# Expert loop of a fused layer: gate transposes ahead of the second-layer pass, and differences that read the largest values in place

## The reference, cut to what matters

```python
z = jnp.einsum('nd,sdr->nsr', xf, P)
scores = jnp.einsum('nsr,smr->nsm', z, C)
topv, topi = jax.lax.top_k(scores, K)
w = jax.nn.softmax(topv, axis=-1)
h = jax.nn.gelu(jnp.einsum('nsr,nskrh->nskh', z, W1g) + b1g)
yl = jnp.einsum('nskh,nskhr->nskr', h, W2g) + b2g
comb = jnp.einsum('nskr,nsk->nsr', yl, w)
out = jax.nn.gelu(comb @ G1 + g1b) @ G2 + g2b
```

## Time and profile before

| what | value |
|---|---|
| three runs | 931.4, 931.75, 930.24 us |
| median | 931.4 us |
| profiled execution: its own time / span in the profile | 930.38 / 928.5 us |
| PE busy | 882.7 us (95%) |
| DVE busy | 676.9 us (73%) |
| ACT busy | 568.1 us (61%) |
| POOL busy | 474.8 us (51%) |
| mean granted TensorE clock | 0.985 |

### The profile page before, as it was taken

How to read it: one execution, slowest core, us unless ns; L and a number is a source line. 1 busy time by engine, 2 the same in 40 slices (tenths; PEclk the granted TensorE clock), 3 DMA queues, 4 the chain that set the end, 5 groups by cost and what they waited for, 6 DMA issues and landing times.

```text
span 928.5 us, 16150 instructions
## 1 busy us (share of the span) xinstructions
PE 882.7 (95%) x5422; PEld 396.3 (43%) x5422; DVE 676.9 (73%) x1681; ACT 568.1 (61%) x844; POOL 474.8 (51%) x445
## 2 busy tenths in 40 slices
PE   8899999999999989899999999999999999899997
PEld 3477777777677756222222222322232222222222
DVE  6566655665576677887787888888878887877674
ACT  1121211124332256888787889788978897888784
POOL 0335353334234524675856485757565757575452
PEclk8999999999999999799999999999999999999999
DMA  9500001000000096777786879788878887889772
GB/s 284 190 1 1 1 1 74 1 1 1 1 1 15 21 156 177 211 229 232 208 269 202 268 228 280 215 257 236 275 218 264 237 269 236 249 242 297 236 253 98
DMA packets 89804, 154.14 MB, mean 166 GB/s; under 512 B 30211, under 2 KB 56068, under 8 KB 89329
## 3 DMA queue, kind: packets, MB, share of 16 engines
q1 hardware_dynamic: 89236, 151.48, 54.2%
q10 hardware_dynamic: 486, 1.62, 1.1%
HBM read 138.81 MB, written 15.83 MB: 167 GB/s over the span
## 4 chain that ended last, share of the span: by engine, by line
PE 70%; ACT 10%; DVE 9%; issue 6%; DMA 3%; POOL 2%; SPq 1%; ACTq 0%; DVEq 0%; POOLq 0%
PE ps L855 14%; PE ps L792 13%; PE ps L496 9%; PE ps L504 5%; PE ps L569 4%; PE ps L831 3%; PE ps L561 3%; DVE ring L1634 3%; PE ps L578 3%; PE ps L539 2%; ACT ring L1180 2%; ACT ring L1169 2%; PE ps L591 2%; DMA wbc<-w_rows 1%; PE ps L622 1%
## 5 line engine op out<-in xcount | busy, mean ns | idle before, releaser
L1832 POOL TENSOR_TENSOR ring<-ring,wbc 128x512 f32<-128x512 f32 x192 | 245.4, 1280 | 168.8 <-ACT ring L1180 156.8
L1631 DVE TENSOR_TENSOR ring<-ps,ring 128x1024 f32<-128x1024 f32 x192 | 234.5, 1221 | 82.6 <-PE ps L831 58.1
L792 PE MATMUL ps<-zst,w1st 99*128 99x512 bf16 x768 | 214.8, 385 | 14.1 <-ACT ring L1169 6.7
L855 PE MATMUL ps<-ring,w2cur 128*32 128x512 f32 x1536 | 205.6, 608 | 0.0
L1169 ACT ACTIVATE ring<-ps 128x1024 f32<-128x1024 f32 x192 | 196.8, 1025 | 3.8 <-PE ps L792 3.7
L1693 POOL TENSOR_TENSOR t<-t 128x768 f32<-128x768 f32 x48 | 87.5, 1837 | 188.8 <-DVE t L1311 188.8
L1182 ACT ACTIVATE ps<-ps 128x512 f32<-128x512 f32 x192 | 113.4, 591 | 61.3 <-PE ps L792 60.7
L1634 DVE TENSOR_TENSOR ring<-ps,wbc 128x512 f32<-128x512 f32 x192 | 130.8, 681 | 0.6 <-DMA wbc<-w_rows 0.6
L792 PEld LDWEIGHTS ps<-zst,w1st 99*128 99x128 bf16 x768 | 60.7, 97 | 146.7 <-issue 40.3
L1309 DVE TENSOR_TENSOR t<-ps,rope 128x768 f32<-128x768 f32 x48 | 45.7, 952 | 106.5 <-PE ps L504 70.3
L1180 ACT ACTIVATE ring<-ps 128x512 f32<-128x512 f32 x192 | 115.6, 602 | 0.0
(11 more groups left out here) (174 smaller groups left out, 1130.6 us busy)
## 6 DMA issues: line engine op xcount, KB each, us to landing
wbc<-w_rows SPq DMA_DIRECT2D x192, 512.0 KB, 5.3
w2cur<-in_w SPq DMA_DIRECT2D x48, 256.0 KB, 4.3
w_parts<-wp SPq DMA_DIRECT2D x72, 64.0 KB, 3.1
zst<-z_parts SPq DMA_DIRECT2D x72, 64.0 KB, 4.6
wst<-w_parts SPq DMA_DIRECT2D x24, 128.0 KB, 3.8
z_parts<-zp SPq DMA_DIRECT2D x6, 384.0 KB, 5.6
wst<-w_parts SPq DMA_DIRECT2D x24, 96.0 KB, 3.9
out_h<-h SPq DMA_DIRECT2D x12, 192.0 KB, 5.1
```

Of the source, the lines that this page charges most:

```text
L792: return pe.matmul(bank(to), w1st[0:99, 4 * a + j, col:col + P], zst[0:99, (i // 2) % 2, j, :], start=True, stop=True)
L855: mm = pe.matmul(bank(YBANK, 0, 512, 32 * j, 32 * j + 32), w2cur[:, n, j, :], ring[:, (4 * g + j) % RING, :], start=False, stop=(n == 7 an ...
L1631: dve.tensor_tensor(v, ps[:, WBANK * 512:WBANK * 512 + 1024], v, ALU.mult).then_inc(s["duo_done"], 1)
L1832: pool.tensor_tensor(ring[:, slot, :], ring[:, slot, :], wbc[:, g % 4, 1, :], ALU.mult).then_inc(s["tri_done"], 1)
```

## The change

Two edits. On PE, in the loop, the two places that call `turn_gates` are put ahead of `second(g-2)`; the transpose of normalised rows in block 3 stays behind it. On DVE the copy to `top4` is dropped, with its semaphore step, so `t_top` counts two steps per tile; POOL's differences read `top8[:, :, 0:4]` instead of `top4`.

```diff
@@ sbuf
-        top4 = sb("top4", [P, S, TOPK])
@@ tensor, loop over g
                 if g + 1 < GROUPS:
                     duo_firsts(g + 1)
                     tri_first(g + 1)
-                if g >= 2 and g % 16 != 2:
-                    second(g - 2)
-                if i == 3 and n == 0:
-                    pe.wait_ge(s["wT_done"], tile)
-                    turn_x2(2 * i + 4, PBANK)
                 if i == 0 and n == 5:
                     pe.wait_ge(s["s_copied"], tile + 2)
                     turn_gates(tile, PBANK)
...
                     if n == 7:
                         pe.wait_ge(s["wT_done"], tile)
                         turn_gates(tile, PBANK)
+                if g >= 2 and g % 16 != 2:
+                    second(g - 2)
+                if i == 3 and n == 0:
+                    pe.wait_ge(s["wT_done"], tile)
+                    turn_x2(2 * i + 4, PBANK)
@@ vector, largest
                 ins.then_inc(s["t_top"], 1)
-                dve.wait_ge(s["t_top"], tile * 3 + 1)
-                dve.tensor_copy(top4[:, :, :], top8[:, :, 0:TOPK]).then_inc(s["t_top"], 1)
-                dve.wait_ge(s["t_top"], tile * 3 + 2)
+                dve.wait_ge(s["t_top"], tile * 2 + 1)
                 dve.memset(top8[:, :, TOPK:8], FILLER).then_inc(s["t_top"], 1)
@@ vector, mark
-                    dve.wait_ge(s["t_top"], tile * 3 + 3)
+                    dve.wait_ge(s["t_top"], tile * 2 + 2)
@@ gpsimd, distances
-                pool.wait_ge(s["t_top"], tile * 3 + 3)
+                pool.wait_ge(s["t_top"], tile * 2 + 2)
                 pool.wait_ge(s["s_copied"], tile + 1)
                 pool.tensor_tensor(dist_of(tile)[:, 0:S * M].rearrange("p (s m) -> p s m", m=M), sc[:, :, 0:M],
-                                   _last(top4[:, :, 0], M), ALU.subtract)
-                pool.tensor_tensor(dist_of(tile)[:, S * M:].rearrange("p (s k) -> p s k", k=TOPK), top4[:, :, :],
-                                   _last(top4[:, :, 0], TOPK), ALU.subtract).then_inc(s["p_dist"], 1)
+                                   _last(top8[:, :, 0], M), ALU.subtract)
+                pool.tensor_tensor(dist_of(tile)[:, S * M:].rearrange("p (s k) -> p s k", k=TOPK), top8[:, :, 0:TOPK],
+                                   _last(top8[:, :, 0], TOPK), ALU.subtract).then_inc(s["p_dist"], 1)
```

## The result

The changed kernel takes 923.56 us in the median of four runs (918.24 to 926.36), the kernel before 931.58 in the same runs (930.24 to 932.7). The ratio is 0.9891, 95% interval 0.9865 to 0.9918. Timed again later it was 920.27 against 933.79, ratio 0.9858 (0.9827 to 0.9888). It is faster, by 1.1 to 1.4%; forecast were 921.0 and 1.1%.

What follows compares the result with a forecast made beforehand. PE leads the loop, but at gate transpositions the chain goes through ScalarE and in four places through VectorE's copy. Transposes 3.8 plus copy 6.6 make 10.4 us, so 921.0 from 931.4, own range 918.0 to 924.0, chance 0.64.

Steps and rivals of the forecast that it cites:

- The transposes: Moving them ahead of the second pass gives 17 × 0.27 = 4.6 us, minus 0.8 in block 2: 3.8 us.
- 0.27 per site: At each gate transposition the chain through ScalarE takes 2.16 us against 1.89 on PE alone; the difference comes back whole.
- PE's own order: Cost on PE of the new instruction order at the moved transposes: bounded by ±0.1 us per site, taken as 0.
- wn at n=7: POOL's wn, read by the transposes, has 0.29 us of slack in block 10 and moves along by some 0.5.
- Block 2: Here wn is late, so the second pass runs after the wait instead of before it: 0.8 us lost.
- The copy: Dropping VectorE's copy to top4 takes its waits for POOL off the chain: 6.6 us in all.
- The four long ones: Copies in blocks 5, 9, 13 and 17, which end with POOL's product: 1.22 us back each, 4.9 together.
- The short copies of blocks 7, 11 and 15: Copies of 0.18 us in these blocks and block 1: removal gives 0.2 us each, 0.8 for the four.
- rival B: The memset that stays inherits the wait for POOL, so the copy's part is 2.1 us: 925.5; chance 0.10.
- Rival A: ScalarE's early start is given back, only the copy counts, and block 2 loses 0.8: 925.6 us; chance 0.12.
- Rival C: Next to nothing gained, 1 to 2 us, because a DMA turns up behind both edits: 930; chance 0.09.
- Rival D: Slower through the granted clock: nine more even blocks get a 1.2 GHz stretch, 1.7 us each: 936.3; chance 0.05.

Runs made afterwards that it cites:

- wn first: Both edits, and in block 2 at n=6 POOL makes wn before the normalised rows; 914.77 against 932.24, ratio 0.9820, the lowest of all.
- after: The changed kernel with both edits, in its first timing and profile, against the kernel before: 923.56 against 931.58 us, ratio 0.9891.
- both_again: The changed kernel with both edits, timed and profiled once more against the kernel before: 920.27 against 933.79 us, ratio 0.9858.
- both_padded: Both edits with an unused tensor in the place of top4, so addresses are those of the kernel before: 919.95 us, ratio 0.9863.
- before_shifted: The kernel before with top4 allocated last, so other tensors lie where the changed kernel has them: 933.64 against 933.67, ratio 0.9998.

## Why the prediction was right, step by step

**The transposes: mechanism right, size off.** The 0.27 per site by way of ScalarE came back whole: the chain no longer leaves PE. In addition the new order costs PE less, 0.44 instead of 0.60. I had bounded that term by ±0.1 and taken 0; it is -0.16, outside the bound. By the gates' starts on PE, block 10 with the move alone has 2.85, 2.29 and 2.73 for groups 5 to 7 where it had 3.00, 2.56 and 2.87, and the next group 2.29 for 2.56: 0.83 for two sites, 0.42 per site. 17 sites make 7.1, not 4.6: this is the first term that was too small, and the 0.16 of PE's own order that I put at 0 is the reason. Less 1.0 for block 2 that is 6.1; the move alone measured 0.63%, 5.9 us. Its profile had a stretch at 1.2 GHz behind the long wait too.

**wn at n=7: right.** With 0.29 of slack it moved along with the gelu; PE waited for POOL in the loop once, in block 2.

**Block 2: right in mechanism, and half of its cost not seen.** The pass without cover cost 1.0 (forecast 0.8). A stretch at 1.2 GHz added about 1.0 in the same block, and one in block 4 comes and goes with the new order. I had put such stretches down as a rival and as ±1.7 in the range. Between 445 and 457 us one began in all four profiles with the long wait in block 2, in four of the seven with the old order there, and in neither of the two with wn first. The long wait may favour it; it isn't needed for it, and thirteen profiles don't settle it. The best version still had one in block 4.

**The copy: right in the places, too small in the count.** The four long ones gave 1.18 per block with the copy alone, for 1.22 forecast (with both edits 1.46, 0.27 of it from the transposes in front). The short copies of blocks 7, 11 and 15, for which I took 0.2 each, were short only where a late load of wbc had shifted POOL; with one of 1.27 in each of the three the removal is worth 3 us more. 6.6 plus that is 9.6; the copy alone measured 0.97%, 9.1 us. This is the second term that was too small. One profile showed one side of a race between two engines; the timed runs may hold both.

**The memset (rival B): refuted.** 85 ns in all 24, also inside POOL's product. **Rival A: refuted** by the move alone, 0.9937. **Rival C** in small: in the profile of the changed kernel two loads of wbc end waits, and blocks 7 and 20 are 0.8 and 0.65 longer than before; in the repeat these two are 19.4 and 20.1. **Rival D** in part: in all three profiles of both edits alone (after, both_again, both_padded) there are two stretches in blocks 2 to 4, where before had one and before_shifted none.

**Why the total still came out near 921.** In part by luck. Both terms of the sum were too small, 3.8 against 5.9 measured alone and 6.6 against 9.1. The four executions of the first timing gave 8.0 us by the medians, the six of the next 13.5; the forecast's 10.4 lies between. In the profiled execution two errors had opposite signs: the loop gave more (11.8) and the hand-over was 7.0 later, for which no tie to the change was found: the first product stood between 369.8 and 378.0 in thirteen profiles, at 371.0 and 373.9 in the two with all instructions of the kernel before, and at 374.0 and 378.0 in the two of the changed kernel. About 3 of the 7.0 are the store of z_parts: it took 6.7 to 7.9 us in six of the eleven profiles with all the loads queued, with the first product at 373.9 or earlier, and 9.4 to 9.8 in the other five, with the first product at 374.0 or later. The hand-over may be why single times of one kernel lie 2.5 to 9 us apart, but the timed runs don't show it, and the clock is a rival: in the repeat the mean granted clock was 0.988 in the run of 915.33 and 0.981 in the two of 924.5. The profile of before had the second-earliest start among those eleven, and its copies in blocks 7, 11 and 15 were short; so its 930.38 was a favourable draw, and the medians of before in the later timings, 932.2 to 933.8, are higher.

What stays open: what decides how long the store of the gates and z_parts take; it was only shown that it isn't the addresses, that the store waits behind the weight loads (5.9 and 7.0 us with half of them moved), and that moving half of these later loses. Nor is it shown what in the reduction keeps it clear of POOL. Whether the half-clock stretches could be avoided wasn't tried.

## What to carry to other kernels

Put a small producer ahead of a long pass whose result nobody waits for, if its input is ready by then; look for the one site where the input is late, because there the long pass loses its cover, and reorder the input's engine rather than the pass. If a short instruction's duration varies by a factor of seven, look for a wait inside the duration: find what the other engine runs at that moment, and drop the operation by reading in place, or try another one that gives the same bytes. When two engines race, one profile shows one outcome: look for what shifted one of them, here a late load, and price both.

## What the hardware showed that I had not expected

- Four fp32 128x128 transposes cost PE 0.44 us between bf16 matmuls and an fp32 pass, and 0.60 between the fp32 pass and the bf16 gates, the same instructions on the same data.
- A VectorE copy of 32 elements per partition took 0.18 to 1.27 us, a maximum over an axis of one element on the same data 0.185 to 0.189, also inside POOL's TENSOR_TENSOR; next to POOL's TENSOR_SCALAR the copy mostly took 0.18 too.
- A DMA of 64 KB took 16 to 18 us behind the 18 weight loads in eight of the profiles, 12.9 to 15.4 in three, and 5.9 and 7.0 with nine of the loads moved away; a 512 KB one took 16 us while those nine were being loaded.
